# A vision tower with routed experts on one core: new orders on all engines between the embedding and the experts

## The chip, the cores and the metric

One Trainium2 chip, one core. The metric is device time in microseconds (us) of one execution of the kernel; lower is better.

## The reference, cut to what matters

64 images of 4x96x96 are cut into 9 patches of 4096 values each, 576 tokens. One block follows:

```
y = layernorm(patches, ln1_g, ln1_b) @ W_proj + b_proj        # 4096 -> 192
h = layernorm(y, ln2_g, ln2_b)
xs = layernorm(h)[..., :96]
q = (cos(xs) * cos(theta)) as 12 heads of 8                   # per image of 9 tokens
h = h + softmax(q q^T / sqrt(8)) q  @ W_combine.T
x = layernorm(h)
w, idx = softmax(top2(x @ router_w.T))                        # 8 experts, 2 a token
out = h + sum over the two experts e: w_e * (silu(x @ Wg[e].T) * (x @ Wu[e].T)) @ Wd[e].T
```

Everything is float32, and the layer norms have no other parameters than those named.

## The kernel before, in words

**Tiles.** The tokens lie in TILES = 5 tiles of 117 (13 images of 9) with a 118th column of ones, and in two groups: tiles 0 to 2 and tiles 3 and 4 (`GROUPS`). The patch values lie across partitions as KT = 32 blocks of 128.

**Embedding.** For each tile `embed` (TensorE, L1209) multiplies the raw patches by the gain-weighted projection; the norm is applied afterwards, from the mean (an extra column) and the mean of squares. For the latter ScalarE squares four blocks at a time (`squares`, L651), NG = 8 times a tile; `square_add` on VectorE (tiles 1, 2, 4; L964) or `square_adds` on GpSimd (tiles 0, 3; L507, folding L509) adds them up in a running sum, and `square_sum` (TensorE, L1220) sums over partitions. A tile's data have two buffers, so `load_x` on ScalarE's queue (L673) fetches tile t+2 when tile t is done with.

**`front(g)`** on VectorE (L1005 to L1043) does both norms, the third norm and the range reduction for the cosine; ScalarE's `cosine_of` (L678, L680) follows, VectorE multiplies by cos(theta) into `qp` (L1046).

**Attention** goes tile by tile over four engines: `turn_queries` (TensorE, L1229), `turned` (ScalarE, L691), `scores` (TensorE, L1240, L1244), `attend` (ScalarE, exponential, L698), `weigh` (TensorE, L1259), `weighed_out` (ScalarE, L707), `turn_back` (TensorE, L1267), `weighed` (VectorE, L1056, L1057), `turn_outputs` (TensorE, L1272), `outputs` (ScalarE, L714), and for a whole group `project` (TensorE, L1278) and `normed` (VectorE, L1067 to L1073). scores(t) needs the score banks free, so it waits for attend(t-1). `keep_busy` (L1196) are matmuls whose result nobody reads.

**Routing.** `turn_normed`, `rows`, `route`, `choose` (L1082 to L1095) find the two experts of a token. One matmul with `before` ranks each token within its expert. GpSimd then works out, in a linked chain of some 40 small instructions (L540 to L591, each waits for the last through `link`), the weights and slots; `meta`, `word` and `posi` are its results. `shares` (VectorE, L1166, L1167) gives the first weight.

**Experts.** The tokens of an expert are handled in chunks of 128 slots: chunks 0 to 7 are the first 128 of each expert, gathered by matmuls with one-hot matrices (`pick` on VectorE, `turn_rows` on TensorE, L1395); chunks 8 to 15 take the overflow rows, which `scatter_rows` (GpSimd, indirect DMA, L598) writes to a DRAM buffer `slot_x` and SyncE reads back. Unused slots of `slot_x` must hold zero rows and a spare row number, the blank slots. Each chunk has three steps of 256 hidden columns, 48 in all: `gate_up` (L1428 to L1433), `silu` (ScalarE, L815), `gate` (VectorE, L1139), `turn_hidden` (L1440), `hidden_high` and `hidden_low` (L819, L1144), `down` (L1454 to L1456). `finish` (ScalarE, L840) weights a chunk, and `add_out` (GpSimd, indirect DMA with addition, L612) adds it to the output, each after the one before has landed; four buffers (`YB`).

**Weights in two parts.** Each of 64 pieces of the expert weights (eight an expert, 128x528 floats) is loaded by SyncE into a ring of STAGES = 7 buffers (`load_pieces`, L422), rounded to half precision by ScalarE (`high_parts`, L667: the high part), and the difference is rounded to bfloat16 by GpSimd or VectorE (`take_rest`, L408: the low part), called through `rests`. The sixteen pieces in `VEC_PIECES` are VectorE's, the others GpSimd's. Load n waits for the low part of piece n-7. Chunk c needs pieces up to 8c+7. Pieces of experts 4 to 7 lie where the embedding kept its data.

**What sets the order.** Every engine runs one list written out by hand, in order: the calls at the end of each engine's section. In the experts' loop ScalarE takes one high part a step from step 2 on, beginning with `high`:

```
            high = 48
            for n in range(NSTEP):
                ...
                silu(n)
                if n >= 1:
                    hidden_high(n - 1)
                ...
                if n >= 2 and high < NP * E:
                    high_parts(high, high + 1)
                    high += 1
```

A function of ScalarE such as sine, exponential or silu needs its table; the compiler puts a load (ACT_TABLE_LOAD) ahead of the first use.

## Time and profile before

| what | us |
|---|---|
| median of three runs | 242.29 (241.88 to 242.65) |
| the profiled execution, its device time | 243.7 |
| its span in the trace | 241.9 |
| busy: TensorE matmul | 201.7 (83%) |
| VectorE | 144.2 (60%) |
| GpSimd | 136.9 (57%) |
| ScalarE | 126.5 (52%) |
| DMA, mean over the span | 150 GB/s |

The span is what the profile draws; the device time holds 1.8 us more around it. A wait is put down to what ended it. In rows a first number is the start in us from the span's start, a second the length.

### The profile page before, as it was taken

The page shows a single profiled execution, that of the slowest core. Times are in us where ns is not written, and L with a number is a line of the kernel's source. Part 1 is how long each engine was busy: PE and PEld are TensorE (multiplying, and loading weights), DVE is VectorE, ACT ScalarE, POOL GpSimd, SP SyncE. Part 2 cuts the span into 40 slices and gives each one's busy share as a digit, 9 for nine tenths or more (in the row PEclk, how much of TensorE's full clock was granted, in tenths as well). Part 3 has the DMA queues.
Part 4 walks back from the last instruction along what each step waited for, and adds up shares of the span by engine and source line. Part 5 has one row for each costly group of instructions (what it writes and reads, how often), then busy time and mean ns, then how long its engine had stood idle before and what let it go on. Part 6 is the DMA issues. An engine that isn't in the chain of part 4 may idle for free.

```text
span 241.9 us, 4779 instructions
## 1 busy us (share of the span) xinstructions
PE 201.7 (83%) x1576; PEld 152.6 (63%) x1576; DVE 144.2 (60%) x421; ACT 126.5 (52%) x288; POOL 136.9 (57%) x183
## 2 busy tenths in 40 slices
PE   0798999699997879558949997977879999999960
PEld 0798989699994546245524774744556767766740
DVE  3899957399559521668234768747963554455430
ACT  0524665769579757508825665445453444444430
POOL 7796554399999701002972888888852223332222
PEclk9999999979999999957897999999999999999995
DMA  6999999993278720420653422655243112222221
GB/s 206 424 426 289 415 322 401 305 373 130 59 226 244 199 83 3 133 80 12 180 157 104 120 57 59 148 190 175 39 103 78 18 19 39 41 38 41 19 30 17
DMA packets 19089, 36.29 MB, mean 150 GB/s; under 512 B 3674, under 2 KB 9082, under 8 KB 18554
## 3 DMA queue, kind: packets, MB, share of 16 engines
q1 hardware_dynamic: 15689, 27.43, 36.3%
q0 software_dynamic: 2944, 2.76, 7.7%
q10 hardware_dynamic: 432, 5.80, 5.8%
q8 instruction: 13, 0.21, 0.4%
q14 instruction: 11, 0.08, 0.1%
HBM read 31.63 MB, written 4.36 MB: 149 GB/s over the span
## 4 chain that ended last, share of the span: by engine, by line
PE 40%; POOL 13%; SPq 12%; DMA 10%; ACT 9%; DVE 7%; issue 6%; POOLq 1%; ACTq 0%
DMA stage<-w_exp 9%; POOL experts L408 8%; SPq L422 4%; PE ps L1428 4%; PE ps L1440 4%; PE ps L1429 4%; PE ps L1433 4%; PE ps L1432 4%; PE ps L1430 4%; POOL experts L507 3%; SPq L442 3%; DVE experts L408 3%; PE ps L1454 3%; PE ps L1455 3%; PE ps L1456 3%
## 5 line engine op out<-in xcount | busy, mean ns | idle before, releaser
L408 POOL TENSOR_TENSOR experts<-stage,experts 128x528 bf16<-128x528 f32 x48 | 58.0, 1274 | 43.3 <-ACT experts L667 43.2
L1209 PE MATMUL ps<-experts 128*117 128x193 f32 (+1 forms) x320 | 57.5, 341 | 8.8 <-DVE experts L914 7.7
L1209 PEld LDWEIGHTS ps<-experts 128*117 128x117 f32 (+1 forms) x320 | 55.4, 189 | 9.6 <-issue 8.0
L1139 DVE TENSOR_TENSOR shared<-shared,ps 128x256 f32<-128x256 f32 x48 | 20.1, 419 | 46.4 <-ACT shared L815 46.3
L667 ACT CAST experts<-stage 128x528 f16<-128x528 f32 x64 | 38.4, 632 | 12.0 <-DMA stage<-w_exp 11.9
L815 ACT ACTIVATE shared<-ps 128x256 f32<-128x256 f32 x48 | 18.5, 385 | 33.4 <-PE ps L1433 33.4
L651 ACT ACTIVATE experts<-experts 128x468 f32<-128x468 f32 x40 | 22.7, 590 | 17.8 <-POOL experts L507 8.6
L612 POOL DMA_INDIRECT out<-shared x8 | 12.4, 1545 | 29.7 <-ACT shared L840 27.0
L1454 PE MATMUL ps<-experts,shared 128*128 128x192 f16 (+1 forms) x96 | 23.7, 246 | 1.6 <-DVE shared L1144 1.6
L408 DVE TENSOR_TENSOR experts<-stage,experts 128x528 bf16<-128x528 f32 x16 | 18.5, 1159 | 8.7 <-ACT experts L667 8.6
L1440 PEld LDWEIGHTS ps<-ident,shared 128*128 128x128 f32 x96 | 12.8, 141 | 17.2 <-DVE shared L1139 9.7
L1440 PE MATMUL ps<-ident,shared 128*128 128x128 f32 x96 | 18.8, 277 | 5.9 <-DVE shared L1139 5.9
L1455 PE MATMUL ps<-experts,shared 128*128 128x192 bf16 (+1 forms) x96 | 23.6, 246 | 0.0
L1456 PE MATMUL ps<-experts,shared 128*128 128x192 f16 (+1 forms) x96 | 23.6, 246 | 0.0
L1428 PE MATMUL ps<-experts,shared 128*128 128x512 f16 (+1 forms) x48 | 18.7, 389 | 5.3 <-ACT shared L826 3.7
L507 POOL TENSOR_TENSOR experts<-experts 128x468 f32<-128x468 f32 x14 | 20.4, 1460 | 2.4 <-ACT experts L651 1.5
L1196 PE MATMUL ps<-ones_b,before 128*128 128x512 bf16 x79 | 21.7, 406 | 0.0
L612 POOL DMA_INDIRECT out<-shared,slot_row x8 | 13.3, 1668 | 14.2 <-ACT shared L840 9.4
L1144 DVE TENSOR_TENSOR shared<-ps,shared 128x256 bf16<-128x256 f32 x48 | 20.0, 416 | 1.5 <-ACT shared L819 1.5
L819 ACT CAST shared<-ps 128x256 f16<-128x256 f32 x48 | 17.7, 369 | 4.3 <-PE ps L1440 4.3
L1429 PE MATMUL ps<-experts,shared 128*128 128x512 bf16 (+1 forms) x48 | 18.6, 388 | 0.0
L1433 PE MATMUL ps<-experts,shared 128*128 128x512 bf16 (+1 forms) x48 | 18.4, 384 | 0.0
(223 smaller groups left out, 357.6 us busy)
## 6 DMA issues: line engine op xcount, KB each, us to landing
stage<-w_exp SPq DMA_DIRECT2D x64, 264.0 KB, 3.2
experts<-x_t ACTq DMA_DIRECT2D x3, 1888.0 KB, 10.2
experts<-w_proj SPq DMA_DIRECT2D x4, 768.0 KB, 7.5
experts<-x_t SPq DMA_DIRECT2D x4, 472.0 KB, 8.2
experts<-x_t SPq DMA_DIRECT2D x1, 1888.0 KB, 14.8
slot_x<-experts SPq DMA_DIRECT2D x1, 1032.0 KB, 15.3
shared<-slot_x SPq DMA_DIRECT2D x8, 129.0 KB, 2.4
out<-h SPq DMA_DIRECT2D x1, 351.0 KB
```

What stands on the lines that cost most here:

```text
L408: ops.tensor_tensor(lo_w[:, to + EW:to + EW + PW], stage[:, n % STAGES, :], hi_w[:, to:to + PW], ALU.subtract).then_inc(split_pool if on_p ...
L507: g.tensor_tensor(acc, acc, sq[:, ((NG - 1) * t + j) % 2], ALU.add).then_inc(sq_used_pool, 1)
L612: pool.indirect_dma_start(out=out, out_offset=bass.IndirectOffsetOnAxis(ap=rows, axis=0), in_=yc[:, c % YB, :], in_offset=None, compute_op ...
L667: a.copy(hi_w[:, to:to + PW], stage[:, n % STAGES, :]).then_inc(hi_done, 1)
L1209: last = mm(dst, xbuf[:, t % 2, k, 0:m], gw[:, k, :], start=k == 0, stop=k == KT - 1)
L1428: mm(dst, x1h[:, c % 2, 0, :], part_w(0, off, k1, 2 * BLK), start=True, stop=False)
L1429: mm(dst, x1h[:, c % 2, 0, :], part_w(1, off, k1, 2 * BLK), start=False, stop=False)
L1433: mm(dst, x1h[:, c % 2, 1, :], part_w(1, off, k2, 2 * BLK), start=False, stop=True).then_inc(gu_done, 1)
L1440: last = tr(pcol(4 + n % 2, h * P, P), hid[:, n % 2, h * P:(h + 1) * P], ident[:, :])
L1454: mm(y, hh[:, n % 2, h, :], part_w(0, off, col, D), start=k == 0, stop=False)
L1455: mm(y, hh[:, n % 2, h, :], part_w(1, off, col, D), start=False, stop=False)
L1456: last = mm(y, hl[:, n % 2, h, :], part_w(0, off, col, D), start=False, stop=end)
```

## The change

It sets new orders on all engines between embedding and experts:

- all 64 low parts are GpSimd's; 9 rather than 13 before tile 3's adds, and 52 (`POOL_FIRST`) before the placement chain rather than 44 with eight of VectorE's; the last twelve lie between the scatters and the output additions;
- the blank slots (rows of zeros with the spare number in place) are built in the tail of expert 3's area and written by one transfer, after 16 pieces; SyncE loads 52 pieces before the output's first rows;
- `load_table` runs a one-column activation to have a table loaded ahead: Exp, Sin, Exp, Silu;
- ScalarE's and TensorE's lists are rearranged, `front` loses its last part to `queries`, tile 4's squares are folded by VectorE (`halve`) so that TensorE sums two blocks for four, the gap of the two logits moves from GpSimd to VectorE, `shares` moves ahead of `place`;
- turn_queries(3) writes bank 3, and needs no wait of its own for tile 4.

```diff
+    POOL_FIRST = 52
...
-    VEC_PIECES = (32, 33, 34, 35, 44, 45, 46, 47, 48, 49, 50, 51, 60, 61, 62, 63)
+    VEC_PIECES = ()
...
+blanks = flat[:, EARLY * EW - MORE * ROW:EARLY * EW].rearrange("p (k w) -> p k w", k=MORE)
...
-TURN_BANK = (7, 0, 1, 2, 2)
+TURN_BANK = (7, 0, 1, 3, 2)
...
     sp.dma_start(rt2[:, :], router[P:D, :]).then_inc(consts_in, 16)
-    load_pieces(0, STAGES)
-    sp.wait_ge(pool_consts, 1)
-    slots = slot_x.rearrange("(c p) w -> p c w", p=CHUNK)[:, E:CHUNKS, :]
-    sp.dma_start(slots[:, :, 0:ROW], spread(blank[:, :].rearrange("p (o w) -> p o w", o=1), 1, MORE)).then_inc(blank_out, 16)
-    sp.dma_start(out[NTOK:NTOK + SPARE, :], blank[0:SPARE, 0:D]).then_inc(blank_out, 16)
-    load_pieces(STAGES, 2 * STAGES)
-    sp.wait_ge(blank_out, 32)
-    sp.dma_start(slots[:, :, ROW - 2:ROW - 1].bitcast(i32), spare_row[:, :].rearrange("p (c o) -> p c o", o=1),
-                 allow_slow_non_contiguous=True).then_inc(blank_out, 16)
-    load_pieces(2 * STAGES, 50)
+    load_pieces(0, 2 * STAGES + 2)
+    sp.wait_ge(blank_ready, 1)
+    sp.dma_start(slot_x[E * CHUNK:CHUNKS * CHUNK, :].rearrange("(p k) w -> p k w", k=MORE), blanks).then_inc(blank_out, 16)
+    sp.dma_start(out[NTOK:NTOK + SPARE, :], blanks[0:SPARE, 0, 0:D]).then_inc(blank_out, 16)
+    load_pieces(2 * STAGES + 2, 52)
     sp.wait_ge(h1_kept, len(GROUPS))
     for a, n, rows in ((0, TILES - 1, TOK), (TILES - 1, 1, LAST)):
         sp.dma_start(out[a * TOK:a * TOK + n * rows, :].rearrange("(t p) d -> p t d", p=rows),
                      h1[0:rows, a:a + n, :]).then_inc(out_base, 16)
-    load_pieces(50, NP * E)
+    load_pieces(52, NP * E)
...
     square_adds(0)
-    rests(0, 13)
+    g.memset(blanks[:, :, :], 0.0)
+    pool.wait_ge(pool_iota, 1)
+    link(g.tensor_scalar(eighth[:, :], validi[:, 0:1], MORE / CHUNK, 0.5 * MORE / CHUNK - 0.5, ALU.mult, ALU.add))
+    link(g.tensor_scalar(eighth[:, :], eighth[:, :], MAGIC, None, ALU.add))
+    link(g.tensor_scalar(eighth[:, :], eighth[:, :], MAGIC, -float(CHUNK), ALU.subtract, ALU.mult))
+    g.tensor_scalar(blanks[:, :, ROW - 2].bitcast(i32), spare_no[:, :], eighth[:, 0:1], None, ALU.add).then_inc(blank_ready, 1)
+    rests(0, 9)
     square_adds(3)
     for t in range(TILES):
         for k in range(2):
             g.iota(xs[:, t, k, ROW - 2:ROW - 1].bitcast(i32), pattern=[[0, 1]], base=t * TOK, channel_multiplier=1)
-    rests(13, 40)
+    rests(9, 46)
     low_parts(0)
-    rests(40, 41)
+    rests(46, 48)
     low_parts(1)
-    rests(41, 44)
-    pool.wait_ge(hot_ready, len(GROUPS))
-    g.tensor_tensor(gap[0:TOK, :], top[0:TOK, :, 1], top[0:TOK, :, 0], ALU.subtract).then_inc(gap_ready, 1)
+    rests(48, POOL_FIRST)
     pool.wait_ge(place_ready, 1)
...
-    pool.wait_ge(blank_out, 48)
+    pool.wait_ge(blank_out, 32)
     pool.wait_ge(xs_ready, len(GROUPS))
     pool.wait_ge(out_base, 32)
+    scatter_rows(0, 3)
+    rests(POOL_FIRST, 56)
     add_out(0)
-    rests(52, 54)
-    scatter_rows(0, 2)
+    scatter_rows(3, 6)
+    rests(56, 58)
     add_out(1)
-    rests(54, 56)
-    scatter_rows(2, 4)
+    scatter_rows(6, 10)
+    rests(58, 62)
     add_out(2)
-    rests(56, 58)
-    scatter_rows(4, 7)
-    rests(58, 60)
-    add_out(3)
-    scatter_rows(7, 10)
-    add_out(4)
-    for c in range(5, CHUNKS):
+    rests(62, 64)
+    for c in range(3, CHUNKS):
         add_out(c)
...
+            if n == NP * (EARLY - 1):
+                sc.wait_ge(blank_out, 32)
             if n == NP * EARLY:
                 sc.wait_ge(tok_done, TILES)
                 sc.wait_ge(ssq_done, TILES)
-                sc.wait_ge(blank_out, 48)
                 sc.wait_ge(vec_consts, 1)
             sc.wait_ge(stage_in[n % STAGES], 16 * (n // STAGES + 1))
...
+    def load_table(kind):
+        a.activation(preload[:, :], halfpi[:, :], kind)
...
@@ ScalarE
     load_x(2)
     for j in range(NG):
         squares(1, j, j + 1)
-        if j >= 3:
+        if 3 <= j <= 5:
             high_parts(j - 3, j - 2)
-    high_parts(5, 7)
+    high_parts(3, 4)
     sc.wait_ge(tok_done, 2)
     a.copy(c1_row, ps[ONE_Q:TOKX, emb_at(0):emb_at(0) + D]).then_inc(c1_ready, 1)
     load_x(3)
+    high_parts(4, 5)
     for j in range(NG):
         squares(2, j, j + 1)
-        if j in (3, 5, 7):
-            high_parts(7 + j // 2 - 1, 7 + j // 2)
+        if j in (3, 6):
+            high_parts(4 + j // 3, 5 + j // 3)
     theta_angle = [ps[0:TOK, 4 * BANK + i * Q:4 * BANK + (i + 1) * Q] for i in range(2)]
     cosine(0, ctheta[0:TOK, :], theta_angle[1], theta_angle[0])
-    high_parts(10, 13)
-    squares(3, 0, 3)
-    load_x(4)
+    high_parts(7, 10)
+    for j in range(NG):
+        squares(3, j, j + 1)
+        if j >= 2:
+            high_parts(8 + j, 9 + j)
+        if j == 6:
+            load_x(4)
+    high_parts(16, 20)
+    squares(4, 0, 3)
+    high_parts(20, 22)
+    cosine_of(0)
     for j in range(3, NG):
-        squares(3, j, j + 1)
-        high_parts(10 + j, 11 + j)
-    squares(4, 0, 3)
-    high_parts(18, 20)
-    cosine_of(0)
-    squares(4, 3, NG)
-    high_parts(20, 26)
+        squares(4, j, j + 1)
+        high_parts(19 + j, 20 + j)
+    load_table(ACT.Exp)
+    high_parts(27, 30)
     turned(0)
     turned(1)
     turned(2)
-    high_parts(26, 27)
+    high_parts(30, 31)
     attend(0)
-    high_parts(27, 29)
+    high_parts(31, 33)
+    attend(1)
     weighed_out(0)
-    attend(1)
-    high_parts(29, 31)
+    high_parts(33, 34)
+    attend(2)
     weighed_out(1)
-    attend(2)
+    load_table(ACT.Sin)
+    high_parts(34, 35)
     cosine_of(1)
     weighed_out(2)
+    load_table(ACT.Exp)
     turned(3)
+    turned(4)
     outputs(0)
     outputs(1)
-    turned(4)
     outputs(2)
     attend(3)
-    high_parts(31, 33)
+    high_parts(35, 37)
+    attend(4)
     weighed_out(3)
-    attend(4)
-    high_parts(33, 35)
+    high_parts(37, 38)
     weighed_out(4)
-    high_parts(35, 36)
+    high_parts(38, 40)
     outputs(3)
     outputs(4)
+    high_parts(40, 42)
     rows(0)
     keep_h1(0)
     both_choices(0)
-    high_parts(36, 42)
+    high_parts(42, 47)
     rows(1)
     keep_h1(1)
     both_choices(1)
-    high_parts(42, 45)
+    high_parts(47, 51)
     sc.wait_ge(gap_ready, 1)
     a.activation(gexp[0:TOK, :], gap[0:TOK, :], ACT.Exp).then_inc(gexp_ready, 1)
-    high_parts(45, 48)
+    load_table(ACT.Silu)
+    high_parts(51, 52)
...
         a.activation(yc[:, c % YB, :], pcol(Y_BANKS[c % 2], 0, D), ACT.Copy, scale=w).then_inc(y_ready, 1)
     rows_high(0)
-    high = 48
+    high = 52
...
+    def halve(t):
+        wait_added(dve, t, NG - 1)
+        v.tensor_tensor(ssq[:, t % 2, 0:2], ssq[:, t % 2, 0:2], ssq[:, t % 2, 2:4], ALU.add).then_inc(ssq_halved, 1)
...
         v.scalar_tensor_tensor(left, near, -MAGIC, turns, ALU.add, ALU.subtract).then_inc(left_ready, 1)
+    def queries(g):
+        t0, t1 = GROUPS[g]
+        emb = in_bank(g, 0, D + 1, t1 - t0)
+        own = lambda t, w: emb[:, t - t0, 0:w]
         dve.wait_ge(cos_ready, g + 2)
...
@@ VectorE, the list
+    def gap_of_top():
+        dve.wait_ge(hot_ready, len(GROUPS))
+        v.tensor_tensor(gap[0:TOK, :], top[0:TOK, :, 1], top[0:TOK, :, 0], ALU.subtract).then_inc(gap_ready, 1)
     front(0)
-    for j in range(1, NG):
+    for j in range(1, 3):
         square_add(4, j)
+    queries(0)
+    for j in range(3, NG):
+        square_add(4, j)
+    halve(4)
     front(1)
     weighed(0)
+    queries(1)
     weighed(1)
     weighed(2)
-    rests(32, 34)
     normed(0)
     weighed(3)
-    rests(34, 35)
     weighed(4)
-    rests(35, 36)
     normed(1)
     choose(0)
     choose(1)
+    gap_of_top()
...
+    def shares():
+        dve.wait_ge(gexp_ready, 1)
+        link(v.tensor_scalar(wsel[0:TOK, 2, :], gexp[0:TOK, :], 1.0, None, ALU.add))
+        v.reciprocal(wsel[0:TOK, 0, :], wsel[0:TOK, 2, :]).then_inc(share_ready, 1)
...
     pick(0, chosen[:, :, 0:1])
+    shares()
     v.tensor_copy(place[:, :, :].rearrange("p t e -> p (t e)"), pcol(6, 0, te + E)).then_inc(place_ready, 1)
...
-    def shares():
-        dve.wait_ge(gexp_ready, 1)
-        link(v.tensor_scalar(wsel[0:TOK, 2, :], gexp[0:TOK, :], 1.0, None, ALU.add))
-        v.reciprocal(wsel[0:TOK, 0, :], wsel[0:TOK, 2, :]).then_inc(share_ready, 1)
...
     for n in range(NSTEP):
         c, r = divmod(n, STEPS)
         gate(n)
         if n >= 1:
             hidden_low(n - 1)
-        if n == 0:
-            shares()
         if r == 1 and E <= c + 1 < CHUNKS:
             rows_low(c + 1)
         if r == 1 and c + 2 < E:
             pick(c + 2, slot_val[0:TOK, :, c + 2:c + 3])
         if r == 2 and 1 <= c <= E:
             slot_facts(c - 1)
-        if r != 1 and c < 4:
-            rests(44 + 2 * c + r // 2, 45 + 2 * c + r // 2)
-        if c in (5, 6) and r != 1:
-            rests(60 + 2 * (c - 5) + r // 2, 61 + 2 * (c - 5) + r // 2)
     hidden_low(NSTEP - 1)
 @block.tensor
...
-        if vec_ssq(t):
+        if t == 4:
+            pe.wait_ge(ssq_halved, 1)
+        elif vec_ssq(t):
             wait_added(pe, t, NG - 1)
         else:
             pe.wait_ge(ssq_ready_pool, tiles_before(t) + 1)
-        terms = GS if vec_ssq(t) else 2
+        terms = 2 if t == 4 or not vec_ssq(t) else GS
         for i in range(terms):
             last = mm(ps[0:TOK, ssq_at(t):ssq_at(t) + 1], ssq[:, t % 2, i, :], mean_k[:, 0:1], start=i == 0, stop=i == terms - 1)
         last.then_inc(ssq_done, 1)
...
     def turn_queries(t):
         pe.wait_ge(q_ready, group_of(t) + 1)
-        if t == 4:
-            pe.wait_ge(qT_ready, t)
...
@@ TensorE, the list
     embed(2, KT - KC, KT)
     square_sum(2)
     embed(3, 0, KT)
+    square_sum(3)
     embed(4, 0, KT)
-    square_sum(3)
     square_sum(4)
     pe.wait_ge(consts_in, N_CONSTS)
     turn_queries(0)
     turn_queries(1)
     turn_queries(2)
-    keep_busy(3, 5)
     scores(0)
-    keep_busy(7, 8)
+    keep_busy(7, 5)
     scores(1)
     weigh(0)
-    keep_busy(7, 3)
+    keep_busy(7, 2)
+    scores(2)
     turn_back(0)
-    scores(2)
     weigh(1)
-    keep_busy(7, 3)
     turn_back(1)
     weigh(2)
-    keep_busy(3, 3)
+    keep_busy(5, 2)
     turn_back(2)
-    keep_busy(3, 6)
+    keep_busy(5, 4)
     turn_queries(3)
+    turn_queries(4)
     turn_outputs(0)
     turn_outputs(1)
-    turn_queries(4)
     turn_outputs(2)
-    keep_busy(3, 3)
     scores(3)
     project(0)
-    keep_busy(7, 6)
+    keep_busy(7, 2)
     scores(4)
     weigh(3)
     keep_busy(7, 3)
+    weigh(4)
     turn_back(3)
-    weigh(4)
-    keep_busy(3, 3)
+    keep_busy(3, 1)
     turn_back(4)
-    keep_busy(3, 3)
+    keep_busy(3, 2)
     turn_outputs(3)
     turn_outputs(4)
-    keep_busy(3, 2)
+    keep_busy(3, 1)
     project(1)
+    keep_busy(6, 3)
     turn_normed(0)
+    keep_busy(6, 3)
     route(0)
-    keep_busy(6, 10)
+    keep_busy(6, 2)
     turn_normed(1)
-    keep_busy(6, 4)
+    keep_busy(6, 3)
     route(1)
-    keep_busy(6, 10)
+    keep_busy(6, 8)
...
```

## Rows read from the trace of the kernel before

**Rows 1.** The page: a group of instructions, and a DMA with its us to landing.

```profile
L408 POOL TENSOR_TENSOR experts<-stage,experts 128x528 bf16<-128x528 f32 x48 | 58.0, 1274 | 43.3 <-ACT experts L667 43.2
...
stage<-w_exp SPq DMA_DIRECT2D x64, 264.0 KB, 3.2
```

**Rows 2.** Timeline of TensorE, embedding: start us, length us, instruction, [idle before].

```profile
46.70 0.98 PE L1220 MATMUL ps<-mean_k,experts 128*117 128x1 f32 x8 [1.84 <-DVE experts L964]
47.54 22.91 PE L1209 MATMUL ps<-experts 128*117 128x193 f32 x128
```

**Rows 3.** Windows: busy us of PE, PEld, DVE, ACT, POOL; granted clock, DMA share, GB/s.

```profile
49.00:50.00 1.00, 1.00 (x5) 0.99 (x4) 0.86 (x6) 1.00 (x3) 1.00 (x2) 0.50 1.43 461
```

**Rows 4.** Timeline of SyncE's queue, the issue behind the blank slots' write.

```profile
22.80 8.14 SPq L442 DMA_DIRECT2D out<-experts  x1
```

**Rows 5.** Timeline of ScalarE, attention and experts.

```profile
75.13 1.28 ACT L698 ACT_TABLE_LOAD   x1
76.43 1.34 ACT L698 ACTIVATE experts<-ps 117x1404 f32<-117x1404 f32 x1
...
83.68 1.35 ACT L698 ACTIVATE experts<-ps 117x1404 f32<-117x1404 f32 x1
...
161.42 0.63 ACT L667 CAST experts<-stage 128x528 f16<-128x528 f32 x1 [3.25 <-DMA stage<-w_exp]
```

**Rows 6.** Timeline of VectorE, from `front(1)` to the experts.

```profile
71.68 0.16 DVE L1005 COPY small<-ps 117x2 f32<-117x2 f32 x1 [1.99 <-PE ps L1220]
...
82.15 0.36 DVE L1043 SCALAR_TENSOR_TENSOR ps<-whole,ps 117x192 f32<-117x192 f32 x1
...
99.42 0.76 DVE L1067 TENSOR_TENSOR ps<-h,ps 117x576 f32<-117x576 f32 x1
...
104.25 0.22 DVE L1056 RECIPROCAL rden<-ps 117x12 f32<-117x12 f32 x1
...
108.60 0.56 DVE L1067 TENSOR_TENSOR ps<-h,ps 117x384 f32<-117x384 f32 x1 [1.92 <-PE ps L1278]
...
147.72 3.65 DVE L408 TENSOR_TENSOR experts<-stage,experts 128x528 bf16<-128x528 f32 x1
...
163.04 2.61 DVE L1119 TENSOR_TENSOR yy<-slot,slot_val 117x640 f16<-117x640 f32 x1
```

**Rows 7.** Timeline of GpSimd.

```profile
6.05 1.70 POOL L501 MEMSET shared<- 128x1920 f32 x1
...
52.16 8.74 POOL L507 TENSOR_TENSOR experts<-experts 128x468 f32<-128x468 f32 x7
...
62.31 18.79 POOL L408 TENSOR_TENSOR experts<-stage,experts 128x528 bf16<-128x528 f32 x16
...
113.41 4.62 POOL L408 TENSOR_TENSOR experts<-stage,experts 128x528 bf16<-128x528 f32 x4 [17.63 <-ACT experts L667]
...
121.52 3.48 POOL L408 TENSOR_TENSOR experts<-stage,experts 128x528 bf16<-128x528 f32 x3
...
131.18 0.57 POOL L543 TENSOR_TENSOR wsel<-wsel,gexp 117x5 f32<-117x5 f32 x1 [5.80 <-DVE wsel L1167]
...
145.63 0.32 POOL L591 COPY xs<-wsel 117x5 f32<-117x5 f32 x2
...
166.82 0.98 POOL L598 DMA_INDIRECT slot_x<-xs,posi  x1 [0.30 <-issue]
```

**Rows 8.** Timeline of TensorE, `gate_up`'s first matmul of a step.

```profile
127.56 0.58 PE L1428 MATMUL ps<-experts,shared 128*128 128x512 f16 x1 [3.73 <-ACT shared L826]
...
146.76 0.38 PE L1428 MATMUL ps<-experts,shared 128*128 128x512 f16 x1
...
160.62 0.38 PE L1428 MATMUL ps<-experts,shared 128*128 128x512 f16 x1
...
163.68 0.38 PE L1428 MATMUL ps<-experts,shared 128*128 128x512 f16 x1
...
187.38 0.39 PE L1428 MATMUL ps<-experts,shared 128*128 x1
```

10 lines of the change are left out of this document (6 added, 4 removed).

## The prediction

> **What bounds the kernel now.** I read the page first: no engine is full, and the low parts are the largest group [rows 1]. So I followed, stage by stage, which wait ends last. *Embedding*: TensorE works without a break but for 1.84 us before tile 2's sum of squares; tiles 3 and 4 then take 22.91 us [rows 2], part of it at the lower clock (granted 0.50, that is 1.2 GHz, after that pause) [rows 3]. SyncE's queue stands 8.14 us in one issue behind the blank slots' write [rows 4]. *Attention*: the three first exponentials start 3.63 us apart (76.43 to 83.68, two steps), with a table load of 1.28 us before the first [rows 5]. *Before the experts*: VectorE's `rests(32, 34)` wait for ScalarE's high parts, so `normed(0)` starts at 99.42 and `normed(1)` at 108.60 [rows 6], while GpSimd sits idle for 17.63 us before 113.41; GpSimd then does low parts until 125.00 and only then the gap, on which ScalarE's exponential waits [rows 7]. ScalarE's `rows_high(0)` stands behind it, and the first expert matmul starts at 127.56, 3.73 us idle [rows 8]. *Experts*: chunks 0 to 2 take 19.20 us, 6.4 a chunk, a pause at the lower clock included; at that pace, with 5.9 for chunk 7 (its successor needs no gathering matmuls), eight take 50.7. They take 59.8 (127.56 to 187.38) [rows 8]: 9.1 us are stalls, where VectorE's low part and pick last 3.65 and 2.61 us [rows 6] and ScalarE waits 3.25 us for a piece [rows 5]. From 187.38 to the end of the span are 54.5 us.
>
> **The change, part by part.** The stage ring ties the engines: load n waits for the low part of n-7, lands 3.2 us after its issue [rows 1], and ScalarE takes pieces in order. With SyncE's wait I count 3.5 us from a low part to the piece seven later.
>
> *Blank slots.* One write in place of two, from a zeroed strip of expert 3, later in the queue. The 8.14 us issue goes; what it delayed was pieces 7 and up, and tile 3's data. GpSimd pays a memset of 2064 columns (1920 take 1.70 us [rows 7]: 1.8) and four small operations (estimate 1 to 3 us in all), mostly while it waits for ScalarE; I count nothing, 1 to 2 us if that cover is gone. ScalarE no longer stops squares(1) for piece 3.
>
> *Tile 2.* With only two high parts between squares(2), its last add comes before its matmuls end (46.70-1.84 = 44.86 [rows 2]). The 1.84 us pause goes: `front(0)` 2 us earlier, tile 3 starts at 45.5.
>
> *Tile 3 and the loads.* GpSimd does 9 rather than 13 low parts before square_adds(3). Low part 8 ends about 45.2; seven adds at 1.25 (8.74/7) and the folding end at 54.6 instead of 61.6 [rows 7]. Tile 4's load now stands behind squares(3, 6), that is four adds: issued at 50.3, landing near 57; TensorE finishes tile 3 about 56.4, so nothing is lost (up to 4 us if the load shares the queues with the blank write). Embedding ends near 68, 2.4 us sooner.
>
> *Tile 4's squares: worse.* Low part 9 can start only at 55.4. From there GpSimd runs at 1.174 a part (18.79/16) [rows 7], piece 16 lands at 60.1, piece 19 at 63.6. `squares(4, 0, 3)` and `cosine_of(0)` stand behind pieces 19 and 21, the last square behind 25: three squares, two parts, cosine 0.9, five squares with four parts between at 0.53 to 0.59 end at 72.8; add and halving 73.9; square_sum(4) 74.5. `front(1)` starts at 74.6, against 71.68 [rows 6]: 2.9 us late. TensorE idles from 68 to 74, and after a shorter pause its clock fell [rows 3]: 1.0 us for the transposes and scores that follow (bounds 0 and 2.5).
>
> *Attention.* Exp is loaded during that wait, and attend(1), attend(2) no longer stand behind the preceding turn back: attend(0) at 78.3, then steps of 1.35 for the exponential, 0.14, 1.0 scores and 0.2, thus 2.7 us instead of 3.63, so attend(2) ends at 84.8 against 85.03 (83.68+1.35) [rows 5]. `front(1)` ends at 85.4, its 10.8 us (71.68 to 82.51) unchanged [rows 6]; cosine_of(1), behind weighed_out(1), the Sin load (1.28) and a high part, at 88.1. So a table load moved ahead of a chain on ScalarE hides only where ScalarE waits: at Exp and Silu yes, at Sin no. attend(3) ends 93.7, attend(4) 96.3. VectorE has no low parts left: normed(0) at 93.5 to 98.4 (4.8 as now: 99.42 to 104.25), weighed(3) and (4) 99.6, 2.5 us of transposes and projection: `normed(1)` at 101.8, **6.8 us sooner**.
>
> The Trainium skill (ScalarE: Activation LUTs, What ACT_TABLE_LOAD costs) gives about 1.28 us of load and 1.38 of drain for each switch. The trace agrees on the load, but the exponential follows the load of 75.13 at once, at 76.43 [rows 5]. By the page's figure each hidden load would give 1.4 us more; my sum leaves that out.
>
> *Router to first expert.* ScalarE: outputs, high 40 and 41, rows(0) behind the last projection and its transposes at 103.5, with the copies 2.9 us, high 42 to 46 until 109.1, rows(1). GpSimd has low parts 42 to 45 from 107.3 to 112.0; low_parts of both groups take 2.3 together (118.03 to 121.52 less one part of 1.2) [rows 7], with 46 and 47 between: ready 116.9. The routing (choose(1) at 111) is no longer last. turn_rows(0) 0.9, rows_high(0) 0.7, its gexp and the Silu load done before: first expert matmul at 118.5, plus the 1.0 of clock **119.5, against 127.56**: 8.1 us. In this stretch the gap (VectorE now) and shares cost 0.5 beside GpSimd.
>
> *Experts.* VectorE's 12 low parts go, with their collisions. But GpSimd's queue is now: low 48 to 51 until 122.5; placement, 14.8 us (131.18 to 145.95, the wait of 5.80 gone) [rows 7] until 137.6; three scatters at 1.28 (0.98+0.30); and low part 52 at 142.8, counted at 1.27 [rows 1]. Load 59 waits for it and lands at 146.3. ScalarE asks for piece 59 in step 9, at 119.5+19.2+2.1 = 140.8: **a new wait of 5.5 us**. Silu of step 10 is queued behind it, so VectorE's gate and TensorE's transposes wait too. Beside ScalarE's 3.25 us wait at 161.42, TensorE's step took 3.06 (160.62 to 163.68 [rows 8]) where a plain one takes about 1.8, so some 1.9 us are absorbed: 3.6 lost. Piece 63 hangs on low part 56, behind parts 53 to 55, an add_out and three scatters: 153.4, landed 156.9, asked for at 152.2: 4.7, lost 2.8. Part 63, for chunk 7, ends at 170.8, chunk 7 starts at 171.7: no wait. I add 1.0 for the clock after such a pause (bounds 0 and 3.4) and 1.0 for picks that still collide (the one of 2.61 cost TensorE about 1 us; bounds 0 and 4) [rows 6].
>
> The Trainium skill (GPSIMD Engine Reference, Key points) says that GpSimd shares its SBUF interfaces with VectorE, in contention with VectorE instructions of two SBUF inputs. The 3.65 us low part of VectorE beside GpSimd's agrees. It speaks for taking low parts from VectorE, and against filling GpSimd where picks run.
>
> **Sum.** 119.5 + 50.7 + 6.4 + 1.0 + 1.0 = 178.6 for chunk 8 against 187.38; the tail of 54.5 is untouched (add_out's chain, with GpSimd free from 171, keeps ahead). Span 233.1 against 241.9, 8.8 less. The profiled execution took 243.7, so 234.9 for its like; it is 1.4 above the median of 242.29, which becomes **233.5**.
>
> **Rivals.** *A, the ring wait is hidden* (placement or parts quicker than counted, 5 us in all): no 6.4 and 1.0, hence 226.1. For: the 5.80 wait is gone and VectorE disturbs less; against: the placement is a linked chain, each step waits for the last. 0.17. *B, tile 4's lateness isn't absorbed*: the 1.6 us between front(1) and the cosine vanish and TensorE stays at 1.2 GHz through two scores; with GpSimd's rear 4 to 5 us later, 238. For: ScalarE has nothing to spare at 84. 0.13. *C, the tables are still loaded on the chain*, before each function: two times 1.28, 236. 0.05. *D, slower*: GpSimd becomes the bound at chunk 7, where TensorE waits for low part 63. Forecast 170.8 against 171.7; each us beyond costs one us, and past 181 the kernel is slower than before. It needs 12 parts at over 1.8 and scatters and adds at twice their 1.3: 243.5. Against: the scatter row. 0.07. The forecast has 0.58, with 229 to 238 for itself.
>
> **Numbers.** 233.5. The range 226.5 to 239.5 leaves out D and half of A. A measurement of this kernel tells 0.3%, 0.7 us. Faster: the forecast, A, C and most of B, 0.90; same 0.03; slower 0.07.
>
> **What would show it.** Tile 2's pause gone and one load of tile 4 near 50; front(1) later than 71.68 by some 3; attends 2.7 apart; normed(1) near 102 to 103; first expert matmul near 119.5; ScalarE waiting twice for pieces near 141 and 152, GpSimd never idle there; chunk 8 near 178.6. It is wrong if pieces 59 and 63 are there in time, if tile 4 waits for its data, or if TensorE stands before chunk 7.

## The result, and the profile after

The changed kernel takes **231.98 us** (median of 4 runs, 229.04 to 234.31) beside 242.47 us for the kernel before (241.88 to 244.66, 4 runs). The ratio is 0.9511, 95% interval 0.9398 to 0.9625. Measured again later it took 232.27 us, ratio 0.9575 (0.9521 to 0.9630). Ratios and their intervals leave out executions more than 1.5% above the kernel's shortest, the medians hold all (in e3 and f2 below two executions are left for the ratio), so a median and its ratio need not agree. The profiled execution took 232.1 us with a span of 230.3, against a forecast of 233.1 for the span and 233.5 for the median: faster, as forecast.

The page of the changed kernel, its two lines that answer to [rows 1], and its chain of waits:

```profile
L414 POOL TENSOR_TENSOR experts<-stage,experts 128x528 bf16<-128x528 f32 x64 | 75.3, 1215 | 22.7 <-ACT experts L671 22.6
...
stage<-w_exp SPq DMA_DIRECT2D x64, 264.0 KB, 3.1
...
POOL 30%; PE 27%; DMA 14%; ACT 7%; SPq 7%; issue 7%; DVE 4%; POOLq 1%; ACTq 0%; DVEq 0%
```

All 64 low parts are GpSimd's now, and it holds more of the chain that ends last than any other engine.

TensorE in the embedding (answers to [rows 2]):

```profile
44.21 0.88 PE L1255 MATMUL ps<-mean_k,experts 128*117 128x1 f32 x8
44.96 10.74 PE L1242 MATMUL ps<-experts 128*117 128x193 f32 x64
...
56.87 10.76 PE L1242 MATMUL ps<-experts 128*117 128x193 f32 x64 [0.86 <-DMA experts<-x_t]
72.29 0.94 PE L1255 MATMUL ps<-mean_k,experts 128*117 128x1 f32 x4 [4.67 <-DVE experts L979]
```

Tile 2's pause is gone. Tile 3 and tile 4 run one after the other but for 0.86 us, in which TensorE waits for tile 4's data, and then it stands for 4.67 us until tile 4's squares are added. SyncE's queue (answers to [rows 4]) now needs 0.43 us for each blank write, where one took 8.14:

```profile
44.87 0.43 SPq L446 DMA_DIRECT2D slot_x<-experts  x1
45.34 0.43 SPq L447 DMA_DIRECT2D out<-experts  x1
```

Windows (busy us of PE, PEld, DVE, ACT, POOL; granted clock, DMA share, GB/s), the first answering to [rows 3]:

```profile
49.00:50.00 1.00, 1.00 (x8) 1.00 (x7) 0.97 (x5) 0.85 (x3) 0.92 (x2) 1.00 0.52 191
70.00:72.00 2.00, 0.00 (x0) 0.00 (x0) 1.60 (x3) 1.98 (x4) 2.00 (x3) 0.79 0.76 236
72.00:82.00 10.00, 9.71 (x99) 6.95 (x100) 8.07 (x40) 7.73 (x13) 10.00 (x9) 0.50 0.80 232
82.00:86.00 4.00, 4.00 (x49) 2.71 (x49) 2.31 (x10) 2.34 (x4) 1.63 (x2) 0.50 0.70 206
86.00:91.00 5.00, 4.43 (x51) 2.74 (x44) 0.90 (x5) 4.03 (x9) 1.18 (x1) 0.50 0.09 33
```

The lower clock (0.50, 1.2 GHz) has left tile 3 and sits in the attention, behind the 4.67 us of idleness, until 91 us. ScalarE (answers to [rows 5]):

```profile
71.36 1.28 ACT L699 ACT_TABLE_LOAD   x1
...
76.87 1.34 ACT L706 ACTIVATE experts<-ps 117x1404 f32<-117x1404 f32 x1 [0.62 <-PE ps L1277]
80.78 1.34 ACT L706 ACTIVATE experts<-ps 117x1404 f32<-117x1404 f32 x1 [1.52 <-PE ps L1277]
84.75 1.34 ACT L706 ACTIVATE experts<-ps 117x1404 f32<-117x1404 f32 x1 [1.66 <-PE ps L1277]
...
142.50 0.63 ACT L671 CAST experts<-stage 128x528 f16<-128x528 f32 x1 [2.72 <-DMA stage<-w_exp]
152.87 0.63 ACT L671 CAST experts<-stage 128x528 f16<-128x528 f32 x1 [2.80 <-DMA stage<-w_exp]
```

The exponentials wait for TensorE's scores, and two pieces are late in the experts. VectorE (answers to [rows 6]):

```profile
73.34 0.16 DVE L1029 COPY small<-ps 117x2 f32<-117x2 f32 x1 [1.10 <-PE ps L1255]
95.61 0.76 DVE L1097 TENSOR_TENSOR ps<-h,ps 117x576 f32<-117x576 f32 x1 [3.44 <-PE ps L1311]
103.23 0.56 DVE L1097 TENSOR_TENSOR ps<-h,ps 117x384 f32<-117x384 f32 x1 [1.72 <-PE ps L1311]
...
149.36 2.74 DVE L1157 TENSOR_TENSOR yy<-slot,slot_val 117x640 f16<-117x640 f32 x1
```

GpSimd (answers to [rows 7]), with its last output adds, and TensorE's `gate_up` (answers to [rows 8]):

```profile
54.34 28.10 POOL L414 TENSOR_TENSOR experts<-stage,experts 128x528 bf16<-128x528 f32 x24
...
134.85 1.25 POOL L603 DMA_INDIRECT slot_x<-xs,posi  x1 [0.70 <-POOL xs L596]
...
149.07 2.34 POOL L414 TENSOR_TENSOR experts<-stage,experts 128x528 bf16<-128x528 f32 x2
...
185.44 1.54 POOL L617 DMA_INDIRECT out<-shared,slot_row  x1 [2.72 <-DMA out<-shared,slot_row]
189.63 1.54 POOL L617 DMA_INDIRECT out<-shared  x1 [2.65 <-DMA out<-shared,slot_row]
```

```profile
119.22 0.38 PE L1460 MATMUL ps<-experts,shared 128*128 128x512 f16 x1 [0.29 <-ACT shared L845]
...
168.05 0.39 PE L1460 MATMUL ps<-experts,shared 128*128 128x512 f16 x1 [1.73 <-POOL experts L414]
...
173.82 0.38 PE L1460 MATMUL ps<-experts,shared 128*128 x1
...
192.57 0.38 PE L1460 MATMUL ps<-experts,shared 128*128 x1
196.50 0.39 PE L1460 MATMUL ps<-experts,shared 128*128 x1
```

Three stretches hold the result. First expert matmul: 119.22 against 127.56, 8.3 us. From there to chunk 8: 54.6 us against 59.8, 5.2. From chunk 8 to the end: 56.5 against 54.5, 2.0 given back. Together 11.6 us of span, and 241.9 - 230.3 = 11.6.

### The profile page after: what moved, and what is told of

Read it like the earlier page. It is cut to its first block, busy times and chain, and to the rows that moved or that the text cites. A ratio compares the mean times of both kernels' runs of the same rounds, so it can differ in the third digit from the quotient of the medians.

```text
span 230.3 us, 4712 instructions
## 1 busy us (share of the span) xinstructions
PE 198.5 (86%) x1541; PEld 152.6 (66%) x1541; DVE 128.6 (56%) x407; ACT 127.0 (55%) x292; POOL 154.8 (67%) x202
## 4 chain that ended last, share of the span: by engine, by line
POOL 30%; PE 27%; DMA 14%; ACT 7%; SPq 7%; issue 7%; DVE 4%; POOLq 1%; ACTq 0%; DVEq 0%
POOL experts L414 14%; DMA stage<-w_exp 7%; POOL slot_x L603 4%; POOL experts L507 4%; DMA out<-shared 3%; DMA out<-shared,slot_row 3%; ACT experts L653 3%; PE ps L1229 3%; POOL out L617 2%; SPq L428 2%; ACT experts L671 2%; PE ps L1460 2%; PE ps L1277 2%; PE ps L1465 2%; PE ps L1462 2%
## 5 line engine op out<-in xcount | busy, mean ns | idle before, releaser
L414 POOL TENSOR_TENSOR experts<-stage,experts 128x528 bf16<-128x528 f32 x64 | 75.3, 1215 | 22.7 <-ACT experts L671 22.6
L1242 PE MATMUL ps<-experts 128*117 128x193 f32 (+1 forms) x320 | 56.6, 338 | 8.6 <-DVE experts L933 7.7
L1242 PEld LDWEIGHTS ps<-experts 128*117 128x117 f32 (+1 forms) x320 | 54.8, 188 | 9.0 <-DMA experts<-x_t 8.6
L1460 PE MATMUL ps<-experts,shared 128*128 128x512 f16 (+1 forms) x48 | 18.2, 379 | 2.0 <-POOL experts L414 1.7
L1465 PE MATMUL ps<-experts,shared 128*128 128x512 bf16 (+1 forms) x48 | 18.2, 379 | 0.0
L1464 PE MATMUL ps<-experts,shared 128*128 128x512 f16 (+1 forms) x48 | 18.2, 379 | 0.0
L1461 PE MATMUL ps<-experts,shared 128*128 128x512 bf16 (+1 forms) x48 | 18.2, 379 | 0.0
L1462 PE MATMUL ps<-experts,shared 128*128 128x512 f16 (+1 forms) x48 | 18.2, 379 | 0.0
```

The lines of the kernel that those rows point to most:

```text
L414: ops.tensor_tensor(lo_w[:, to + EW:to + EW + PW], stage[:, n % STAGES, :], hi_w[:, to:to + PW], ALU.subtract).then_inc(split_pool if on_p ...
L1242: last = mm(dst, xbuf[:, t % 2, k, 0:m], gw[:, k, :], start=k == 0, stop=k == KT - 1)
L1460: mm(dst, x1h[:, c % 2, 0, :], part_w(0, off, k1, 2 * BLK), start=True, stop=False)
L1462: mm(dst, x1l[:, c % 2, :], part_w(0, off, k1, 2 * BLK), start=False, stop=False)
```

## The experiments

All are read by the same stretches, from each one's profiled execution (us): start of the first `gate_up` (A), from there to chunk 8 (B), and from chunk 8 to the end of the span (C). The last column is B + C less 105.0, which is the least B (50.5) and the least C (54.5) that any run showed. It is what the experts' stage loses. Times are medians. Two executions of one kernel (changed and g1) differ by 0.9 us in A and by 0.8 in B, so smaller differences between single traces say nothing; in C they agree to 0.1.

| kernel | time, ratio to before | A | B | C | lost |
|---|---|---|---|---|---|
| before | 242.5 | 127.6 | 59.8 | 54.5 | 9.3 |
| changed | 232.0, 0.951 | 119.2 | 54.6 | 56.5 | 6.1 |
| g1, the same again | 232.3, 0.958 | 120.1 | 53.8 | 56.5 | 5.2 |
| e1, tables on the chain | 232.9, 0.961 | 120.3 | 54.1 | 56.5 | 5.6 |
| e2, filler in the wait | 228.9, 0.940 | 113.9 | 54.7 | 58.2 | 7.9 |
| e3, squares first | 232.5, 0.959 | 115.6 | 54.6 | 56.8 | 6.4 |
| e4, before with only the low parts moved | 243.4, 1.004 | 120.0 | 66.6 | 54.5 | 16.1 |
| f1, four low parts to VectorE | 230.8, 0.952 | 120.3 | 54.1 | 54.5 | 3.5 |
| f2, low parts ahead of scatters | 234.3, 0.954 | 119.5 | 56.6 | 56.2 | 7.7 |
| f3, old blank write | 236.0, 0.972 | 121.5 | 53.8 | 56.3 | 5.1 |
| f4, e2 and f1 | 227.3, 0.937 | 115.9 | 54.5 | 54.6 | 4.0 |
| g2, f4, one low part at a time | 228.3, 0.942 | 114.2 | 50.5 | 63.1 | 8.6 |
| g3, g2 with adds sooner | 227.5, 0.935 | 115.7 | 55.6 | 54.5 | 5.1 |
| g4, g3 without filler | 232.2, 0.958 | 119.8 | 54.5 | 54.6 | 4.1 |

### e1: the function tables back on the chain

```diff
-            load_table(ACT.Exp)
-            load_table(ACT.Sin)
-            load_table(ACT.Exp)
-            load_table(ACT.Silu)
```

> The changed kernel without its four early table loads; the tables are loaded right before their first use. My account: Exp and Silu were hidden by waits of ScalarE, the second Exp and Sin were not. So attend(0) starts 1.3 us later, as now behind a load of 1.28 us at 76.9, and the load before attend(3) moves behind the turned queries, where it costs up to 1 us; the silu load falls between the first gate_up and silu, at most 1 us, since silu(0) waits for five matmuls. First expert matmul 1 to 2 us later than 119.2, time 1 to 2.5 us above the changed kernel. Rival, early loading does nothing because ScalarE is the bound of that stretch anyway: within 0.5 us. Rival, each switch also costs a drain of 1.4 us: 4 us or more.

232.85 us, ratio 0.9609 (0.9536 to 0.9682), which overlaps the changed kernel's; 0.9 us above it by the medians, where I expected 1 to 2.5. The loads move to 76.61, 88.64, 94.07 and 120.18, each 1.28 us. The first exponential starts at 77.90 where it was 76.87, the fourth at 95.36 where it was 94.41, but `normed(1)` at 103.59 where it was 103.23. The first expert matmul is at 120.31, which g1 (120.07) has with the preloads. So the preloads are worth at most some 0.6 us of span here, and these runs can't tell that from nothing; the rival of 4 us or more is excluded.

### e2: TensorE kept busy while it waits for tile 4's squares

```diff
             embed(4, 0, KT)
+            keep_busy(3, 22)
             square_sum(4)
```

> The changed kernel with 22 more idle matmuls of 512 columns (0.213 us each, 4.7 us) between the last embedding matmul and the sum of squares of tile 4, where TensorE now stands 4.67 us and then works at the granted clock 0.50 from 71 to 82 us. My account: the low clock makes scores, weigh and turn back take twice as long (1.39 against 0.78 us for the 24 matmuls of scores) and stretches the three exponentials from 2.7 to 3.94 us apart. Kept busy, the clock stays at 1.00, attend(2) starts 2.5 to 3 us earlier, but ScalarE's high parts, Sin load and cosine then follow, so normed(1) comes 2 to 3 us earlier and the time falls by 1.5 to 3 us. Rival, GpSimd's low parts are the bound: normed(1) comes earlier, the first expert matmul (119.2) doesn't, and the time is unchanged.

228.92 us, ratio 0.9399 (0.9323 to 0.9476). Windows of e2, and the exponentials and `normed(1)`:

```profile
70.00:72.00 2.00, 2.00 (x10) 0.71 (x8) 1.57 (x3) 1.98 (x3) 2.00 (x3) 1.00 0.77 239
72.00:82.00 10.00, 8.15 (x156) 5.81 (x155) 8.37 (x42) 9.32 (x16) 10.00 (x9) 1.00 0.79 232
```

```profile
75.80 1.36 ACT L706 ACTIVATE experts<-ps 117x1404 f32<-117x1404 f32 x1
78.35 1.34 ACT L706 ACTIVATE experts<-ps 117x1404 f32<-117x1404 f32 x1
80.89 1.34 ACT L706 ACTIVATE experts<-ps 117x1404 f32<-117x1404 f32 x1 [0.32 <-PE ps L1277]
...
97.88 0.56 DVE L1097 TENSOR_TENSOR ps<-h,ps 117x384 f32<-117x384 f32 x1 [1.72 <-PE ps L1311]
```

The clock stays at 1.00 (2.4 GHz), the exponentials stand 2.55 us apart instead of 3.94, and `normed(1)` comes 5.35 us sooner, more than the 2 to 3 that I expected; 0.64 of that is `front(1)`, at 72.70 for 73.34. The wait of 4.67 us therefore cost some 4.7 us of lower clock behind it in this pair of traces. The two later pairs that differ in the filler alone have 3.2 us (f4 and f1: 4.20 at `normed(1)`, 1.00 of it at `front(1)`) and 4.0 us (g3 and g4: 3.16, with `front(1)` 0.85 later). Of the gain in A the experts' stage gives 1.8 back (lost 7.9 for 6.1), all of it in C.

### e3: tile 4's squares right behind piece 15

```diff
-            high_parts(16, 20)
-            squares(4, 0, 3)
-            high_parts(20, 22)
-            cosine_of(0)
-            for j in range(3, NG):
...
+            squares(4, 0, 3)
+            cosine_of(0)
+            squares(4, 3, NG)
+            high_parts(16, 25)
```

> The changed kernel with ScalarE's list altered: squares(4) and cosine_of(0) come right behind piece 15, when tile 4's data have landed (about 57), and pieces 16 to 25 behind them, the later high parts moved by as much. GpSimd is busy with low parts 9 to 15 until 62.5 and needs no high part before. My account says that squares(4) were late because they stood behind pieces 19 to 25 that GpSimd paces: so tile 4's sum is ready before the embedding ends (67.6), front(1) starts at about 68.5 instead of 73.3, TensorE's clock stays at 1.00, normed(1) at about 96 instead of 103.2. GpSimd has then 52 low parts before the placement and is near its bound: from 54.3, 43 parts and the low_parts take 53 us, so the first expert matmul is not before 110; I expect 112 to 114 and a time of 224 to 227. Rival, tile 4's sum is not what orders the stretch (GpSimd is): front(1) earlier, first expert matmul still at 118 to 119, time unchanged.

232.52 us, ratio 0.9589 (0.9523 to 0.9656): missed by 5 us and more. The mechanism came: `front(1)` at 70.29, exponentials 2.6 us apart at clock 1.00, `normed(1)` at 99.65 and A at 115.6, and the profiled execution's span is 227.0. But that trace is of the shortest of four executions (228.8 to 234.2 us), and the interval overlaps the changed kernel's, so what the order is worth stays open.

### e4: the kernel before, with only the low parts moved

```diff
-    VEC_PIECES = (32, 33, 34, 35, 44, 45, 46, 47, 48, 49, 50, 51, 60, 61, 62, 63)
+    VEC_PIECES = ()
```

GpSimd does 44 to 47 behind the gap, 48 to 51 behind the placement and 60 to 63 behind add_out(3).

> The kernel before with one part of the change alone: all low parts on GpSimd, the four of VectorE's before the experts and the twelve within them put into GpSimd's list (44 to 47 behind the gap, 48 to 51 behind the placement, 60 to 63 behind the fourth add_out). My account: normed(0) no longer waits for VectorE's low parts, so normed(1) starts 5 to 7 us before 108.6 and the first expert matmul at 121 to 123 instead of 127.6; in the experts VectorE's long low parts go, but ScalarE waits for pieces that hang on GpSimd's parts behind the placement, as much or more. Time 236 to 240. Rival, the gain comes from the new lists of ScalarE and TensorE alone: normed(1) earlier by less than 2 us, and the time at or above that of the kernel before (242).

243.42 us, ratio 1.0043 (0.9999 to 1.0086); missed, I expected 236 to 240. This part alone brings `normed(1)` from 108.60 to 101.69 and the first expert matmul from 127.56 to 120.00. The whole change has 119.22 and 120.07 (g1), so this part alone gives nearly as much up to the experts as the whole change does. In the experts e4 gives it back, B = 66.6 for 59.8, in two waits, ahead of chunk 7 for the last low part and ahead of chunk 8 for its rows. TensorE's and GpSimd's rows there:

```profile
172.53 0.61 PE L1424 MATMUL ps<-experts,shared 128*128 128x512 f16 x1 [5.70 <-POOL experts L408]
181.65 0.47 PE L1397 MATMUL ps<-ident,shared 128*128 128x128 f32 x1 [3.91 <-DMA shared<-slot_x]
```

```profile
166.21 1.64 POOL L613 DMA_INDIRECT out<-shared,slot_row  x1 [0.17 <-issue]
167.27 5.20 POOL L408 TENSOR_TENSOR experts<-stage,experts 128x528 bf16<-128x528 f32 x4
176.53 1.63 POOL L613 DMA_INDIRECT out<-shared,slot_row  x1 [0.30 <-issue]
```

That is rival D's place, shown: the last low part ends at 172.47, and TensorE stands for it. The last three scatters come behind it, from 172.66 to 176.22, and so do chunk 8's rows. That the order of GpSimd's queue in the change (shares sooner, low parts 48 to 51 ahead of the placement, scatters packed) is what makes the move pay is my reading: the changed kernel has B = 54.6, but it differs from e4 in more than that, and no run takes this order alone.

e4 also shows what the placement chain costs without VectorE's low parts beside it. From the first instruction behind its wait it takes 14.77 us before, 11.90 in e4 (123.62 to 135.52), 12.06 in the changed kernel. One instruction of the chain before, VectorE's low part beside it, and the same instruction in e4:

```profile
134.62 0.75 POOL L557 TENSOR_SCALAR full<-full 128x8 f32<-128x8 f32 x1
134.57 0.70 DVE L408 TENSOR_TENSOR experts<-stage,experts 128x528 bf16<-128x528 f32 x1
...
126.59 0.25 POOL L558 TENSOR_SCALAR full<-full 128x8 f32<-128x8 f32 x1
```

Eight of the chain's instructions are longer so before, each beside a low part or a pick of VectorE.

### f1: low parts 60 to 63 on VectorE

```diff
-    VEC_PIECES = ()
+    VEC_PIECES = (60, 61, 62, 63)
...
+                if c in (4, 5) and r != 1:
+                    rests(60 + 2 * (c - 4) + r // 2, 61 + 2 * (c - 4) + r // 2)
```

> The changed kernel, but the low parts of pieces 60 to 63 are made by VectorE in the gates of chunks 4 and 5, as before the change VectorE made them two chunks later. This takes 4 x 1.2 = 4.8 us off GpSimd between the last scatters and the ring of output adds. My theory: GpSimd's row is what bounds the changed kernel from chunk 7 on, so the wait before chunk 7's first gate_up (1.73 us) and the 1.9 us lost where the output adds run 4.25 us apart behind their backlog both go: 229.0 us (227.5 to 230.5), 3 us below the changed kernel. VectorE's own price: four low parts of up to 3.65 us where they collide, inside chunks whose gates have slack. Rival 1, the collisions decide: each delays a gate by 2 us, TensorE loses it, time 232 to 234. Rival 2, TensorE's columns bound the tail anyway: 231.5 to 232.5.

230.75 us, ratio 0.9515 (0.9470 to 0.9561), 0.25 us above the expected range and not to be told from the changed kernel (g1) by intervals. The trace shows both halves of the expectation: C is 54.5, its 2.0 us are back, and the wait before chunk 7 is gone. B is no shorter, 54.1 for 53.8 in g1: a second pick of VectorE meets GpSimd's low parts now:

```profile
158.59 3.49 DVE L1157 TENSOR_TENSOR h<-slot,slot_val 117x640 f16<-117x640 f32 x1
```

```profile
159.04 2.34 POOL L414 TENSOR_TENSOR experts<-stage,experts 128x528 bf16<-128x528 f32 x2
```

The pick ends at 162.08, 0.70 us behind the low parts' end of 161.38. Undisturbed it takes 0.81.

### f2: low parts 52 to 57 ahead of the scatters

```diff
-            scatter_rows(0, 3)
-            rests(POOL_FIRST, 56)
+            rests(POOL_FIRST, 58)
+            scatter_rows(0, 3)
             add_out(0)
             scatter_rows(3, 6)
-            rests(56, 58)
             add_out(1)
-            scatter_rows(6, 10)
             rests(58, 62)
+            scatter_rows(6, 10)
```

> The changed kernel, with GpSimd's order after the placement turned: low parts 52 to 57 ahead of the scatters, then scatters 0 to 2, add 0, scatters 3 to 5, add 1, low parts 58 to 61, scatters 6 to 9, add 2, low parts 62 and 63. Same work on every engine. ScalarE's two waits for a free stage buffer (2.72 and 2.80 us in the changed kernel) should go or shrink below 1 us each. Theory: these waits are paid out of the same total of GpSimd, so chunk 7 still waits for GpSimd's last low part and the time stays: 232.0 us (231.0 to 233.0). Rival, each of ScalarE's waits is on the path of its chunk: 228.5 us (227.5 to 229.5). Second rival: the output adds pile up more, 233.5 to 235.

234.34 us (229.8 to 237.1), ratio 0.9542 (0.9467 to 0.9617). The median lies in the second rival's range, but the interval overlaps the changed kernel's, so f2 is not shown to be slower. What follows is read from one of its longer executions, of 234.0 us. ScalarE's two waits are gone, as expected: chunks 0 to 4 take 30.75 us, where the changed kernel takes 32.40. By chunk 8 (176.05 for 173.82) more than twice that is paid back: TensorE waits 3.1 us for GpSimd before chunk 7, and one pick stands through a row of four low parts.

```profile
154.37 5.13 DVE L1156 TENSOR_TENSOR h<-slot,slot_val 117x640 f16<-117x640 f32 x1
```

```profile
153.59 5.22 POOL L414 TENSOR_TENSOR experts<-stage,experts 128x528 bf16<-128x528 f32 x4
```

### f3: the old blank write

```diff
-            load_pieces(0, 2 * STAGES + 2)
-            sp.wait_ge(blank_ready, 1)
...
+            load_pieces(0, STAGES)
+            sp.wait_ge(pool_consts, 1)
...
+            load_pieces(STAGES, 2 * STAGES)
+            sp.wait_ge(blank_out, 32)
+            sp.dma_start(slots[:, :, ROW - 2:ROW - 1].bitcast(i32), spare_row[:, :].rearrange("p (c o) -> p c o", o=1),
```

> The changed kernel with the old blank write: a one-partition zero row, three transfers from SyncE, the third waiting for the first two, its words 8 us of issue time in SyncE's queue; all other orders as changed. Theory: the issue holds the piece loads behind it and ScalarE's early high parts by up to 8 us, of which the ring of seven buffers takes most; load of tile 4 was already at 49.3, behind ScalarE's order, so 1 to 2.5 us of it show in the time: 233.6 us (232.5 to 235.0). Rival: it is hidden wholly, 231.7 to 232.5. Other rival: the pause that the kernel before shows ahead of tile 2's squares comes back, 235 to 237.

236.01 us, ratio 0.9724 (0.9678 to 0.9769), against 0.9575 (0.9521 to 0.9630) for the changed kernel in g1: the intervals don't touch, so the new write is worth some 3.7 us, more than the 1 to 2.5 that I expected. The time lies in the range of the other rival, but its mechanism is not there: tile 2's sum of squares starts at 44.05 without a pause. The long issue is that of the second transfer, to `out`, not that of the words. SyncE's queue and tile 4's matmuls:

```profile
22.05 7.73 SPq L450 DMA_DIRECT2D out<-experts  x1
```

```profile
58.85 12.22 PE L1242 MATMUL ps<-experts 128*117 128x193 f32 x64 [2.67 <-DMA experts<-x_t]
```

Tile 4's load is issued at 51.30 instead of 49.34, its matmuls start 2 us later and take 12.22 us for 10.76, `front(1)` is at 74.89 instead of 73.34 and A at 121.5. That is 1.5 to 2.3 us; the profiled execution was this kernel's shortest, and where the rest of the 3.7 goes no trace shows.

### f4: filler and low parts on VectorE together

The edits of e2 and f1.

> The changed kernel with both: 22 more filler products of TensorE while VectorE adds tile 4's squares (as in the second run, which came to 228.9 us), and low parts 60 to 63 on VectorE. Theory: the first gives 5.3 us up to the experts, of which the second run kept 3 to 3.5 because GpSimd's adds then bound the tail; with GpSimd's row 4.8 us shorter nearly all of it is kept: 224.5 us (223.0 to 226.5). Rival: the two gains share one cover and the time is that of the second run, 228 to 229.

227.26 us, ratio 0.9367 (0.9325 to 0.9409), below g1's interval, though it just touches that of the changed kernel's first measurement (from 0.9398). C is 54.6 where e2 alone had 58.2, so the output adds' backlog was what e2 lost. It is 0.8 us above the expected range, because A came at 115.9, not at 113.9 as in e2. B is as long as ever.

### g1 and g2: the changed kernel again, and GpSimd's row cut up

g2 is f4 with this in place of the rows from `scatter_rows(0, 3)` to `rests(62, 64)`:

```diff
+            for n in range(8):
+                rests(POOL_FIRST + n, POOL_FIRST + n + 1)
+                if n in (3, 6):
+                    add_out(n // 3 - 1)
+                else:
+                    scatter_rows(n - (n > 3) - (n > 6), n + 1 - (n > 3) - (n > 6))
+            scatter_rows(6, 10)
+            add_out(2)
```

> The changed kernel itself once more, beside the next one, so that differences of 1 to 2 us between it and its variants can be read: its four times lie between 229.0 and 234.3 us. Expected 231.7 us (231.0 to 232.5); then the variant with low parts 60 to 63 on VectorE (230.8) saves 1 us, the one with the low parts ahead of the scatters (234.3) costs 2.6, and the one with the old blank write (236.0) costs 4. Rival: the changed kernel's times move as a whole with the hour, 233 to 235, and then these differences are smaller or of the other sign.

> The variant with the 22 filler products and low parts 60 to 63 on VectorE (227.3 us), with GpSimd's row after the placement cut up: never more than one low part behind another, each followed by one scatter or one output add, the last scatters behind piece 59. Theory: ScalarE's waits for a free stage buffer (1.94 and 2.22 us there) shrink below 1 us, as where all of 52 to 57 stood ahead; and VectorE's picks, which took 3.4 to 5.1 us where a row of two to four low parts ran beside them and ended 0.7 us behind the row's last, now wait for at most one low part, so none takes over 2.2 us. Together 3 to 4 us of the 54.5 us between the first expert product and chunk 8: 223.8 us (222.5 to 225.5). Rival 1: scatters end later and the load of chunk 8's rows or the output adds lose it again, 226 to 228. Rival 2: a pick waits as long as before because indirect transfers hold VectorE too, picks over 2.5 us, 225.5 to 227.

g1: 232.27 us, as expected, so the changed kernel's median repeats. g2: 228.33 us, ratio 0.9424 (0.9376 to 0.9471), missed. Up to chunk 8 the theory held: no pick in the experts over 1.6 us, VectorE's low parts at most 1.50, ScalarE's waits down to 0.59, B from 54.5 to 50.5. Then rival 1 took all of it and more. TensorE in g2, where it turns the rows of chunk 12:

```profile
183.43 0.38 PE L1461 MATMUL ps<-experts,shared 128*128 x1
190.83 0.45 PE L1434 MATMUL ps<-ident,shared 128*128 128x128 f32 x1 [5.94 <-DMA shared<-slot_x]
192.25 0.64 PE L1461 MATMUL ps<-experts,shared 128*128 x1
```

The load of those rows waits in SyncE's queue for an output add four chunks back (`y_out`), and the adds, 4.2 to 4.6 us apart, were behind: that of chunk 8 starts at 185.09.

### g3: the output adds sooner

```diff
+            for step in ("a0 r52 s0 r53 s1 r54 s2 a1 r55 s3 r56 s4 s5 a2 r57 s6 r58 s7 a3 r59 s8 s9 a4").split():
```

Here a is an output add, r a low part, s a scatter; the rest is f4.

> The run before this one reached chunk 8 at 165.1 us, 50.5 us behind its first expert product where the changed kernel takes 54.6, and lost it again between 184 and 193 us, where TensorE waited for rows whose load waits for an output add. Here GpSimd's order after the placement is: add 0, then low parts and scatters one by one, add 1 behind scatter 2, add 2 behind scatter 5, add 3 behind scatter 7, add 4 behind scatter 9; same fillers, same low parts 60 to 63 on VectorE. Theory: the output adds, 4.2 us apart once they run alone, are what bounds the tail, and only their backlog: here add 5 starts near 164 us where there it was 172.0, so the tail from chunk 8 is 54.5 to 55.5 us and the time 222.0 us (220.5 to 224.0). Rival: the last scatters are later by two adds, so chunk 8's rows come late, 224.5 to 226.5. Rival: the tail is bound by something else than the adds' backlog and stays near 62 us, 228 to 229.

227.49 us, ratio 0.9348 (0.9305 to 0.9391); missed by 3.5 us above its range, though the tail came as expected, C = 54.5. Its adds wait for ScalarE now, not for one another:

```profile
183.39 1.55 POOL L617 DMA_INDIRECT out<-shared  x1 [2.96 <-ACT shared L852]
188.98 1.55 POOL L617 DMA_INDIRECT out<-shared  x1 [4.04 <-ACT shared L852]
```

The price moved to B, 55.6: add 0 stands ahead of low part 52, and ScalarE waits for pieces again, 0.68, 1.94, 2.46 and 0.78 us.

### g4: the same without filler

> The same order of GpSimd without the 22 filler products: the changed kernel with low parts 60 to 63 on VectorE and the adds sooner. If the clock's share is a term by itself, this is later by what the filler gave before: the first expert product near 119.5 us, chunk 8 near 170, time 226.2 us (225.0 to 228.0), against 232.3 for the changed kernel. Rival: with the experts starting later the scatters and adds have more room and the tail is shorter by a further microsecond, 224.5 to 225.

232.22 us, ratio 0.9575 (0.9528 to 0.9621), 6 us above what was expected, and no better than the changed kernel: A came as expected, but chunk 8 at 174.3, not at 170. Against g3 it lacks only the filler: 4.7 us, of which 4.1 are A (119.8 for 115.7). The experts' order alone is worth 1 to 2 us of a profiled span and nothing that these runs can tell.

## Why the prediction came out right, and where its steps did not

**Right, with the mechanism.** VectorE's wait for high parts went, `normed(1)` is at 103.23 (forecast "at 101.8", plus 1.0 of clock), and the first expert matmul at 119.22 (119.5). e4, where only the low parts move, shows what that wait was worth, 6.9 us at `normed(1)`. Tile 2's pause and the 8.14 us issue went; tile 4's load is issued at 49.34 (50.3), `front(1)` comes late, at 73.34 (74.6). GpSimd's blank work, 1.82 us and four small operations of 1.6 together, is hidden, just: its next low part still waits 0.15 us for ScalarE. The undisturbed pace of 50.7 us for eight chunks is what g2 shows, 50.5. The table loads hide where I said and are worth under 1 us. By the Trainium skill (ScalarE: Activation LUTs, What ACT_TABLE_LOAD costs) a switch costs a drain of 1.38 us beside the load, so each hidden one would have saved some 1.4 us more, an estimate from that figure. In e1 three of the four loads stand ahead of `normed(1)`, which is 0.36 us later, and the exponential follows the load of 76.61 at 77.90, so no such drain shows here.

**Mis-sized: the clock.** "1.0 us for the transposes and scores that follow (bounds 0 and 2.5)" measured 3.2 to 4.7 (e2 and the two later pairs), outside its bounds. From 72 to 91 us TensorE was at 1.2 GHz, so the exponentials that I put "2.7 us" apart stood 3.94 apart. The sum stayed right because the chain beside it was too long by about as much: e2, with the clock up, has `normed(1)` at 97.88, not 101.8, and 2.5 of these 3.9 us are there at the first exponential already (75.80 for "attend(0) at 78.3"). Two errors of 2 to 4 us with opposite signs: that the first expert matmul came within 0.3 us of its forecast is luck.

**Mis-sized: ScalarE's waits.** "A new wait of 5.5 us" and "4.7" measured 2.72 and 2.80. The placement took 12.1 us (122.09 to 134.15), not the 14.8 of [rows 7]: I had carried over a length that it had only beside VectorE's low parts (e4). ScalarE asked at 139.8 and 150.1, where I had 140.8 and 152.2, which by itself makes the waits longer, not shorter. The 6.4 + 1.0 + 1.0 us of losses in B measured 54.6 - 50.5 = 4.1, with the chunk 7 wait in it.

**Failed: chunk 7.** "Part 63, for chunk 7, ends at 170.8, chunk 7 starts at 171.7: no wait." TensorE was ready at 166.3 and waited 1.73 us. Part 63 ended at 167.99, 2.8 us sooner than forecast, but TensorE was there 5.4 us sooner, so the margin of 0.9 turned over. e4 shows the same place at 5.70 us. This was named as a sign of being wrong, and so was tile 4 waiting for its data, which it did for 0.86 us.

**Failed: the tail.** "The tail of 54.5 is untouched (add_out's chain, with GpSimd free from 171, keeps ahead)." It took 56.5. GpSimd was free at 168, but the adds are chained: each waits for the one before to land, 4.2 us apart, and they start late because the last low parts stand ahead of them. From 164 to 194 they catch up with chunks 5.6 us apart; the load of a late chunk's rows waits for one of them, and one step of TensorE starts 2 us late (192.57 to 196.50, where steps are 1.8 to 2.0). f1 and f4 move four low parts away and have the 54.5; g2, with the same low parts moved, brings chunk 8 forward but not the adds and has 63.1; g3 has g2's work with the adds sooner, and 54.5. The cost there is when the chain starts and its pace, not the sum of GpSimd's load.

So the experts' stage came to 2.5 us less than forecast (111.1 for 113.6 by span), out of 4.5 too much in B and 2.0 too little in C, and that these partly cancel is luck too. Rival A's forecast of nearly no wait for pieces was half true; rival C is excluded, since the loads stand at 71.36, 87.45, 90.51 and 115.68, ahead of the first uses; rival B's clock came true, its lateness did not; rival D's mechanism is real but small here. Two steps of the forecast's arithmetic are 0.3 us off: attend(2) would end at 85.05 (78.3 + 2 x 2.7 + 1.35), not at 84.8, and the placement at 137.3 (122.5 + 14.8), not at 137.6; neither matters to the result.

What stays open: which part of the new order makes B 54.6 where e4 has 66.6; why f3 loses 3.7 us where its trace shows 2; what e3's order is worth; and whether one order of GpSimd can have both B = 50.5 and C = 54.5, which would be near 222 us with the filler. The best versions run are f4 and g3, 227.3 and 227.5 us, some 2% below the changed kernel.

## What to carry to other kernels

A wait of TensorE ahead of a latency-bound stage cost twice here, its own length and the lower clock behind it; filling it with idle products was worth more (3 to 5 us) than any further order tried on the changed kernel. Where one engine's queue serves three customers (weights for ScalarE's ring, scatters, chained output adds), price each order by all three: f2 and g2 gained 1.7 and 4 us for one customer and lost more for another. Taking four low parts off the queue left the least loss in the traces (3.5 us in f1, for 5.2 and 6.1), though its time alone can't be told from the changed kernel's. A length read from a trace depends on what ran beside it: the placement chain took 14.8 us only beside VectorE's low parts. A chain of transfers that wait for one another has a pace of its own, so it must start early; that the issuing engine is idle says nothing.

## What the runs showed of the hardware that I had not expected

- VectorE's pick (two operands in SBUF) takes 0.81 us alone. Beside GpSimd's low parts it took 2.74, 3.49 and 5.13 us, and each time ended 0.7 us behind the row of low parts (149.36 + 2.74 = 152.10 against 149.07 + 2.34 = 151.41): it seems to stand until the row ends, whether of two or of four. It isn't always so: a pick took 1.76 us beside a row of six (f2) and 1.73 beside a row of four (e4), and ended within the row. With single low parts between scatters the longest was 1.56 in g2 and 2.52 in g4, and a pick that began with a scatter (134.90 in the changed kernel) took 0.82.
- The disturbance goes both ways: in the placement before the change a GpSimd instruction of 0.25 us (e4) took 0.75 beside a low part of VectorE.
- After the 4.67 us pause the granted clock was 0.50 from 72 to 91 us, although TensorE was busy in 9.71 of the first 10 us.
- Output adds by indirect transfer take 1.54 us to issue and 4.2 to 4.3 us from one to the next when each waits for the last to land.
- The blank transfer to `out` held SyncE's queue for 7.73 us in f3 (8.14 before) and for 0.43 in the changed kernel, where it is issued later and behind the other form of the write to `slot_x`. Which of the two matters was not tried.
